# Maxima moved straight from the turned tile into the query rows, and 24 chunks ahead of a group's scores in place of 26

## The reference, cut to what matters

```python
x = x + attn_a(layernorm(x), Wq, bq, Wk, bk, Wv, bv, Wo, bo)
x = x + ffn(layernorm(x), w_gate, w_up, w_down)
x = x + attn_b(layernorm(x), wq, wk, wv, wo)
x = x + ffn(layernorm(x), w_gate, w_up, w_down)

# attn_a: 32 heads of 8 columns, no mask
scores = einsum('bhqd,bhkd->bhqk', q, k) * scale        # scale = 1/sqrt(8)
ctx    = einsum('bhqk,bhkd->bhqd', softmax(scores), v)  # then ctx @ Wo + bo
# attn_b: 32 query heads, 8 heads of keys and values (4 query heads share one)
amask  = where((j >= i - 128) & (j < i), -1e10, 0)      # a masked band
# ffn: silu(x @ w_gate) * (x @ w_up); of each 4 neighbours the 2 largest by size stay; @ w_down
```

## Time and profile before

| | us |
|---|---|
| median of 3 runs | 1660.44 |
| lowest, highest | 1656.22, 1662.11 |
| the profiled execution | 1661.54 |
| its span | 1659.6 |
| PE busy | 1611.3 (97%) |
| VectorE busy | 1490.8 (90%) |
| ScalarE busy | 1282.2 (77%) |
| POOL busy | 267.5 (16%) |
| mean busy share of the DMA queue's 16 engines | 29.2% |

### The profile page before, as it was taken

The page is one execution under the profiler, slowest core; times in us unless marked ns, Lnnn a source line. Parts: engine busy times, 40 slices in busy tenths (PEclk is TensorE's granted clock), DMA queues, the critical chain, the costliest instruction groups (busy, mean ns, idle before and its releaser), DMA issues.

```text
span 1659.6 us, 39596 instructions
## 1 busy us (share of the span) xinstructions
PE 1611.3 (97%) x14128; PEld 638.9 (38%) x14128; DVE 1490.8 (90%) x2168; ACT 1282.2 (77%) x2424; POOL 267.5 (16%) x623
## 2 busy tenths in 40 slices
PE   6899999999999999999988999999999999999999
PEld 3322222222222223777753222222222222247777
DVE  6999999999999997787777999999999999938765
ACT  3399999999999998433224999999999999983321
POOL 1410000000000000000012223333322233320000
PEclk9999999999999999999997999999999999999999
DMA  6943344334354321200404322222223222111000
GB/s 161 295 99 70 63 77 83 63 65 84 68 141 87 71 60 44 64 1 1 117 15 132 64 60 57 51 58 60 55 55 67 63 51 52 55 53 55 14 13 26
DMA packets 72126, 114.70 MB, mean 69 GB/s; under 512 B 12464, under 2 KB 27824, under 8 KB 71984
## 3 DMA queue, kind: packets, MB, share of 16 engines
q1 hardware_dynamic: 71984, 112.63, 29.2%
HBM read 71.96 MB, written 40.63 MB: 68 GB/s over the span
## 4 chain that ended last, share of the span: by engine, by line
PE 56%; DVE 32%; issue 7%; DMA 2%; ACT 1%; SPq 1%; DVEq 0%; POOLq 0%; ACTq 0%
DVE mneg L1305 28%; PE psum L785 18%; PE psum L767 11%; PE psum L737 7%; PE psum L887 6%; PE psum L843 6%; PE psum L848 3%; PE psum L700 2%; PE psum L823 2%; DVE area L1355 1%; PE psum L682 1%; PE psum L720 1%; DMA area<-k_stacks 0%; DVE stats L1198 0%; SPq L461 0%
## 5 line engine op out<-in xcount | busy, mean ns | idle before, releaser
L1055 ACT ACTIVATE area<-psum 128x512 f32<-128x512 f32 x2048 | 1097.2, 600 | 42.1 <-PE psum L767 14.6
L785 PE MATMUL psum<-area 128*32 128x256 f32 x8192 | 655.4, 392 | 0.4 <-POOL area L1567 0.4
L767 PE MATMUL psum<-area 51*128 51x512 bf16 x2048 | 638.9, 385 | 2.4 <-DVE vsb_b L1255 1.4
L1311 DVE CUSTOM_DVE_ANT_0 xn<-psum,band 128x1024 f32<-128x1024 f32 x512 | 588.4, 1235 | 12.6 <-PE psum L737 11.3
L1305 DVE TENSOR_REDUCE mneg<-psum 128x1 f32<-128x1024 f32 x512 | 581.0, 1209 | 7.1 <-PE psum L737 7.1
L785 PEld LDWEIGHTS psum<-area 128*32 128x32 f32 x8192 | 162.0, 108 | 400.9 <-issue 259.2
L737 PE MATMUL psum<-area 48*128 48x512 bf16 x1024 | 301.2, 386 | 8.0 <-DVE mneg L1305 4.6
L767 PEld LDWEIGHTS psum<-area 51*128 51x128 bf16 x2048 | 141.1, 94 | 426.5 <-ACT area L1055 353.6
L737 PE MATMUL psum<-k_max_b,area 48*128 48x512 bf16 x1024 | 292.5, 385 | 6.1 <-DVE mneg L1311 5.0
L1548 POOL TENSOR_TENSOR mparts<-mneg,nought 128x16 bf16<-128x16 f32 x64 | 14.2, 222 | 741.6 <-DVE mneg L1305 500.5
L1100 ACT ACTIVATE area<-psum 128x512 f32<-128x512 f32 x64 | 38.2, 600 | 120.0 <-PE psum L848 119.9
(11 more groups left out here) (89 smaller groups left out, 1096.8 us busy)
## 6 DMA issues: line engine op xcount, KB each, us to landing
ctx_rows<-area SPq DMA_DIRECT2D x64, 256.0 KB, 2.1
area<-q_stacks SPq DMA_DIRECT2D x32, 384.0 KB, 6.8
area<-k_stacks SPq DMA_DIRECT2D x64, 192.0 KB, 5.5
area<-q_stacks_b SPq DMA_DIRECT2D x32, 384.0 KB, 5.2
area<-q_stacks SPq DMA_DIRECT2D x32, 192.0 KB, 4.5
area<-q_stacks_b SPq DMA_DIRECT2D x32, 192.0 KB, 3.5
area<-ctx_rows SPq DMA_DIRECT2D x16, 256.0 KB, 3.9
area<-inv_rows SPq DMA_DIRECT2D x16, 256.0 KB, 4.6
```

Of the source, the lines that this page charges most:

```text
L767: pe.matmul(psum[:, BANK_OF["exp", g, u, head], :], k_st[lo:lo + ROWS + PARTS, buf, 0 if a else head // 2, kt * P:(kt + 1) * P], q_st[lo:l ...
L785: mm = pe.matmul(psum[head * VW:(head + 1) * VW, BANK_OF["ctx", g, qh], cols], vaug[:, buf, kt, head, :], probs[:, u % PRING, head, cols], ...
L1055: act.activation(probs[:, u % PRING, head, :], psum[:, BANK_OF["exp", like, u, head], :], ACT.Exp, scale=SCALE).then_inc(bank_freed, 1)
L1311: dve.tensor_tensor_reduce(band_out[:, c % 2, :], slot, band[:, at:at + SEQ], 1.0, -3.0e38, ALU.add, ALU.max, mneg[:, qh, col:col + 1]).th ...
```

## The change

SHIFT is 4 and TURN 6, so LEAD is 24: 24 chunks ahead of the first score, splits with units 4 and 12, turns with units 6 and 14, chunks in the last group's first four units. The last one or two V projections stand one chunk earlier. `mT` goes into the query rows without DRAM: for each parity one transfer of 24 rows of 128 into three rows of `q_st`. For that, `q_st` is laid out by query half, and the queries' rows are loaded by half, in twice as many transfers (96 increments of `st_loaded` for a group and buffer in place of 64, counted by the same rule). `mrow_stored` and `max_rows` are gone; ScalarE's copy into `mT` waits for `mrow_loaded` of two moves before. `ctx_stored` becomes one semaphore for each half.

```diff
-SHIFT = 3
-TURN = 5
+SHIFT = 4
+TURN = 6
 LEAD = CHUNKS - 2 * SHIFT
...
-        max_rows = dram("max_rows", (2, HALF, 2, PARTS, GH // 2 * BANK), BF16)
...
-        q_st, at = carve(at, [2, GH // 2, SEQ], BF16)
+        q_st, at = carve(at, [2, HALF, GH // 2, BANK], BF16)
...
-        V_CHUNKS = [(1, 5, CPH + 1, CPH + 3, CPH + 5, CPH + 7), (CPH + 3, CPH + 5, CPH + 7, CPH + 8)]
+        V_CHUNKS = [(1, 5, CPH + 1, CPH + 3, CPH + 5, CPH + 6), (CPH + 2, CPH + 4, CPH + 6, CPH + 7)]
...
-                    sp.dma_start(q_st[lo:lo + ROWS, buf, :, :],
-                                 qs[g, par::2].rearrange("a d k t -> (d k) a t")).then_inc(st_loaded[buf], 16)
+                    for qh in range(HALF):
+                        tokens = slice(qh * BANK, (qh + 1) * BANK)
+                        sp.dma_start(q_st[lo:lo + ROWS, buf, qh, :, :],
+                                     qs[g, par::2, :, :, tokens].rearrange("a d k t -> (d k) a t")
+                                     ).then_inc(st_loaded[buf], 16)
...
             def move_max(a, g, buf, qh):
                 n = HALF * (GROUPS * a + g) + qh
                 sp.wait_ge(bank_freed, turn_event(a, g, qh) + 1)
-                if not isinstance(g, int) or n >= 4:
-                    sp.wait_ge(mrow_loaded, 32 * (n - 3))
-                sp.dma_start(max_rows[buf, qh].rearrange("a c (i t) -> (a c i) t", t=P),
-                             mT[:, qh, :]).then_inc(mrow_stored, 16)
-                sp.wait_ge(mrow_stored, 16 * (n + 1))
+                if not isinstance(g, int) or n:
+                    sp.wait_ge(mrow_loaded, 32 * n)
                 for par in range(2):
-                    lo = PAR * par + ROWS
-                    sp.dma_start(q_st[lo:lo + PARTS, buf, :, qh * BANK:(qh + 1) * BANK],
-                                 max_rows[buf, qh, par].rearrange("c (i t) -> c i t", i=GH // 2)
-                                 ).then_inc(mrow_loaded, 16)
+                    lo, rows = PAR * par + ROWS, PARTS * CPH // 2
+                    sp.dma_start(q_st[lo:lo + PARTS, buf, qh, :, :],
+                                 mT[rows * par:rows * (par + 1), qh, :]).then_inc(mrow_loaded, 16)
...
-                          q_st[lo:lo + ROWS + PARTS, buf, head // 2, qh * BANK:(qh + 1) * BANK],
+                          q_st[lo:lo + ROWS + PARTS, buf, qh, head // 2, :],
...
-                    act.wait_ge(mrow_stored, 16 * (n - 1))
+                    act.wait_ge(mrow_loaded, 32 * (n - 1))
...
-                if not isinstance(g, int) or n >= 2:
-                    act.wait_ge(ctx_stored, 16 * (n - 1))
+                if not isinstance(g, int) or G:
+                    act.wait_ge(ctx_stored[qh], 16 * G)
```

More of the change, by code:

```diff
@@ L309, in hybrid_kernel @@
         st_loaded = [sem(f"stack_loaded{i}") for i in range(2)]
-        mrow_stored = sem("mrow_stored")
         mrow_loaded = sem("mrow_loaded")
-        ctx_stored = sem("ctx_stored")
+        ctx_stored = [sem(f"ctx_stored{i}") for i in range(HALF)]
         sums_loaded = sem("sums_loaded")
@@ L377, in hybrid_kernel @@
         w_a = [[wqkvo[0], wqkvo[1], wqkvo[2], wqkvo[3]], [wqo_b[0], wkv_b[0], wkv_b[1], wqo_b[1]]]
-        STACK_DMAS = 64
+        MAX_DMAS, ST_DMAS = 64, 96
         V_EARLY = 2
-        V_CHUNKS = [(1, 5, CPH + 1, CPH + 3, CPH + 5, CPH + 7), (CPH + 3, CPH + 5, CPH + 7, CPH + 8)]
+        V_CHUNKS = [(1, 5, CPH + 1, CPH + 3, CPH + 5, CPH + 6), (CPH + 2, CPH + 4, CPH + 6, CPH + 7)]
         V_TILES = BT // len(V_CHUNKS[1])
@@ L402, in stored, with loads @@
             return SD * SLOT[:pairs].count(slot)
-        def loads(G, buf):
-            return STACK_DMAS // 2 * (G - buf) + STACK_DMAS
+        def loads(G, buf, each):
+            return each // 2 * (G - buf) + each
         block = ctx.enter_context(nc.Block())
@@ L536, in move_max @@
                 sp.wait_ge(bank_freed, turn_event(a, g, qh) + 1)
-                if not isinstance(g, int) or n >= 4:
-                    sp.wait_ge(mrow_loaded, 32 * (n - 3))
-                sp.dma_start(max_rows[buf, qh].rearrange("a c (i t) -> (a c i) t", t=P),
-                             mT[:, qh, :]).then_inc(mrow_stored, 16)
-                sp.wait_ge(mrow_stored, 16 * (n + 1))
+                if not isinstance(g, int) or n:
+                    sp.wait_ge(mrow_loaded, 32 * n)
                 for par in range(2):
-                    lo = PAR * par + ROWS
-                    sp.dma_start(q_st[lo:lo + PARTS, buf, :, qh * BANK:(qh + 1) * BANK],
-                                 max_rows[buf, qh, par].rearrange("c (i t) -> c i t", i=GH // 2)
-                                 ).then_inc(mrow_loaded, 16)
+                    lo, rows = PAR * par + ROWS, PARTS * CPH // 2
+                    sp.dma_start(q_st[lo:lo + PARTS, buf, qh, :, :],
+                                 mT[rows * par:rows * (par + 1), qh, :]).then_inc(mrow_loaded, 16)
             def store_ctx(a, g, qh):
                 sp.wait_ge(bank_freed, ctx_event(a, g, qh) + 1)
-                sp.dma_start(ctx_rows[a][g, :, :, qh * BANK:(qh + 1) * BANK], ctx_sb[:, qh, :]).then_inc(ctx_stored, 16)
+                sp.dma_start(ctx_rows[a][g, :, :, qh * BANK:(qh + 1) * BANK], ctx_sb[:, qh, :]).then_inc(ctx_stored[qh], 16)
             def group(a, g, buf, first=False, ahead=2):
@@ L633, in _ @@
                     group(a, 2 * i + 2, 0)
-                sp.wait_ge(ctx_stored, 16 * (HALF * (GROUPS * a + GPB) + 1))
+                sp.wait_ge(ctx_stored[0], 16 * (GROUPS * a + GPB + 1))
+                sp.wait_ge(ctx_stored[1], 16 * (GROUPS * a + GPB))
                 load_sums(a, 0)
@@ L647, in _ @@
                 store_ctx(a, GROUPS - 1, 1)
-                sp.wait_ge(ctx_stored, 16 * HALF * GROUPS * (a + 1))
+                for qh in range(HALF):
+                    sp.wait_ge(ctx_stored[qh], 16 * GROUPS * (a + 1))
                 load_sums(a, 1)
@@ L729, in max_scores @@
                 if c == 0:
-                    pe.wait_ge(max_loaded[buf], loads(GROUPS * a + g, buf))
+                    pe.wait_ge(max_loaded[buf], loads(GROUPS * a + g, buf, MAX_DMAS))
                     if in_feed(a, g, c):
@@ L761, in scores @@
                 if head == 0 and u == 0:
-                    pe.wait_ge(st_loaded[buf], loads(GROUPS * a + g, buf))
+                    pe.wait_ge(st_loaded[buf], loads(GROUPS * a + g, buf, ST_DMAS))
                 if head == 0 and kt == 0:
@@ L1067, in copy_ctx @@
             def copy_ctx(a, g, qh, like):
-                n = HALF * (GROUPS * a + g) + qh
-                act.wait_ge(pv_done, UNITS * (GROUPS * a + g) + (qh + 1) * BT)
-                if not isinstance(g, int) or n >= 2:
-                    act.wait_ge(ctx_stored, 16 * (n - 1))
+                G = GROUPS * a + g
+                act.wait_ge(pv_done, UNITS * G + (qh + 1) * BT)
+                if not isinstance(g, int) or G:
+                    act.wait_ge(ctx_stored[qh], 16 * G)
                 act.copy(ctx_sb[:, qh, :], psum[:, BANK_OF["ctx", like, qh], :]).then_inc(bank_freed, 1)
@@ L1092, in silu_and_size @@
                 if c == 0 and h == 0:
-                    act.wait_ge(ctx_stored, 16 * HALF * GROUPS * (f + 1))
+                    for qh in range(HALF):
+                        act.wait_ge(ctx_stored[qh], 16 * GROUPS * (f + 1))
                 for r in range(5):
```

## The result

The changed kernel takes 1663.79 us (median of 22 runs, 1661.08 to 1665.81), the kernel before 1661.01 us beside it (22 runs, 1656.22 to 1662.57). The ratio is 1.0020, 95% interval 1.0014 to 1.0026: 2.8 us slower. The interval leaves 1 out, so the kernel is slower, by less than the 0.3% from which the prediction would have called it a difference. Forecast were 1660.9 us and a range of 1655.5 to 1666.5. The profiled execution has a span of 1663.1 us and a mean granted clock of 0.986 (before: 1659.6 and 0.989).

The account below looks back on a forecast made before the run. VectorE's unbroken stream of maxima was taken to bound the first attention, with its end behind VectorE's division. First attention +1.25 and second -0.75 made +0.5 us: 1660.9 us against the median, range 1655.5 to 1666.5.

Parts of the forecast that it names:

- The bounding engine: Middle of the first attention: VectorE's 479 maxima run without a hole, 542.04 of 542.05 us; their start sets the end.
- Start of the first attention: First score 0.87 us earlier, but chunk 33 at 92.7, so the stream of maxima is 1.25 us late.
- until the clock returns at 90.7: First attention's start: TensorE runs at 1.96 us a step at the lower clock until 90.7.
- End of the first attention: Stream, inverse, split and division move by +1.25 us; TensorE waits longer at unit 10, nothing is gained: +1.25 us.
- Second attention: Earlier first score and inverse's load, one unit less at the end: -0.75 us, bounds -3.5 and +1.5.
- My account of the inverse's load: Second attention's end: load issued at 1462.5 behind one transfer in place of two, allowing the tile at 1468.45.
- The move: Maxima into the query rows: 3.62 us from turn to landing, 4.6 us of room, 1.0 left; costs nothing.
- The query rows by half: Loads in each group: up to 7 us more of transfer, hidden at both bounds; 0 taken.
- B: Attention starts: the clock returns earlier or does not fall; -1.75 us in the first, total 1657.9 or 1655.2; chance 0.20.
- C: Steady groups: the move misses unit 8 or unit 0 and TensorE stalls; likely +7 us, 1668; chance 0.14.
- D: Both attentions' ends: the unit's gain reaches both, first not held by the division; -0.95 and -0.75, 1658.7; chance 0.08.

Follow-up runs that it names:

- second pair: Kernels after and before, each executed once more unchanged for a second trace: 1662.48 and 1660.45 us.
- after's second trace: The changed kernel executed once more, unchanged: 1662.48 us.
- after with the earlier division: The changed kernel with the first division of the context ahead of the last two of eight weight-splitting operations: 1658.48 us, ratio 0.9993.
- first pair: First traces of the unchanged kernels after and before, with spans of 1663.1 and 1659.6 us.
- before with the earlier division: The kernel before with the first division of the context ahead of the last two of eight weight-splitting operations: 1658.24 us, ratio 0.9981.
- the move alone: The changed kernel with 26 chunks ahead again, keeping the direct move and loads by half: 1660.47 us, ratio 1.0002.
- the two hops: The kernel before with 24 chunks ahead, the maxima still moved through DRAM: 1697.41 us, ratio 1.0219.

## Why the prediction was right in its range, and where its sum was not

The measured 1663.79 us lies in the range of 1655.5 to 1666.5, which the rivals had made wide, and inside the forecast's own 1658 to 1664. The loss of 2.8 us was forecast as 0.5, and the sum held less well than the range.

**The bounding engine** was read rightly: the stream of 479 maxima stands unchanged, moved as a whole.

**Start of the first attention.** First score 78.45 forecast, 78.47 measured; first exponential 80.2 and 80.24; unit 2 at 83.5 and 83.73; steps of 1.96 and 1.98 us. Chunk 33 was forecast for 92.7; it came at 94.50 in one execution and 92.18 in the other. The step "until the clock returns at 90.7" was a fixed number for something that isn't fixed. The size of 1.25 us seems to hold in the second pair (1.44), but that is luck: 0.89 us of it stood between the two executions beforehand. Measured from the copy of V behind chunk 21 the stream is late by 3.13 us where the stretch is 13.7 us long and by 0.44 and 0.22 where it is 6.8 (after's second trace, after with the earlier division); no trace of after has the 10.2 us that the forecast assumed.

**End of the first attention.** This is the step that failed: a term put at nothing. I wrote that TensorE waits for the division at unit 10 "only longer (1.31 + 2.26 us)" and that nothing more follows. The wait was right, 3.57 forecast and 3.22 and 3.20 measured. But I gave it no price beyond itself, and it has one: the granted clock falls to the lower level in the last microsecond of the wait and stays there for 6.8 us, which puts the end of the attention 2.45 us later than the tile in the first pair (5.39 - 2.94) and 2.48 in the second (3.74 - 1.26). Without this term the two pairs, measured from the copy of V, are +1.0 and -1.2 us, around my +0.5, but that is partly luck: the start gave +3.13 and +0.44 in place of +1.25, and the second attention -2.01 and -1.60 in place of -0.75. The earlier division, which takes the wait away, takes the stretch away too. The Trainium skill, "TensorE: Matmul & The Clock Gate", section What's actually happening, has the rule that I had cited for one direction alone: the low clock is the default and activity releases it. By it a longer wait is a risk in itself, and these traces agree: at this place 1.2 to 1.3 us of waiting left the clock alone, 2.50 and 3.2 us did not.

**Second attention.** -0.75 forecast, -2.01 and -1.60 measured. The unit less at the end was worth 2.36 us in the first pair (2.10 forecast): from the end of the stream to the last product with V it is 30.22 us (1461.93 to 1492.15) where it was 32.58. The stream was late by 0.35 us in place of 1.35, since the first score came 1.68 us sooner after the first attention's end (227.15 us against 228.83) and not 0.6; the second pair has the same 227.15 against 228.86. Before shows 6.8 us of low clock at 875.7 just ahead of it, after 3.4 at 882.6, in both pairs. Two other traces have it the other way round: before with the earlier division has 3.4 us of it and 227.89 us to the first score, after with the earlier division has 6.8 us and 228.21. So the lead is worth 0.6 to 0.7 us here (228.83 to 228.21, 227.89 to 227.15), as forecast, and the other 0.9 to 1.1 us go with the stretch and aren't the change's. Where the stretches are alike, all from the first attention's end on gives 0.1 to 0.5 us (821.70 against 822.18 and 821.82) and 0.3 (820.17 against 820.47), less than my 0.75. My account of the inverse's load was wrong: I had it issued at 1462.5, behind one transfer in place of two, and it is issued behind the move of the maxima, as before, at 1467.12. The division ended at 1472.78 and TensorE was there only at 1473.32, so that the error cost nothing.

**The move.** 3.62 us forecast from the turn to the last landing, 3.3 to 3.5 measured; room 4.6 and 4.64; nobody waits. The Trainium skill's 512 bytes ("DMA: Bandwidth & Descriptors", section Specifications) spoke against rows of 256 bytes ending in SBUF. No price of it can be seen: the move alone has the time of before, 1.0002 (0.9993 to 1.0012).

**The query rows by half.** 0 forecast, 0 by the same run. My upper bound was taken from the wrong row: the 384 KB of the earlier trace rows are the loads for the maxima, which the change leaves as they are (6.8 us before, 7.0 after). The loads that were halved had 192 KB and landed after 4.5 us; now they have 96 KB and land after 3.3. The pages of before and after, issues (KB each, median us to landing):

```profile
area<-q_stacks SPq DMA_DIRECT2D x32, 192.0 KB, 4.5
...
area<-q_stacks SPq DMA_DIRECT2D x64, 96.0 KB, 3.3
```

**The rivals.** B (the clock comes back sooner) is what the first start looks like in after's second trace, 6.8 us in place of 10.2, and not in its first, 13.7. The stream gained nothing by it (0.44 us late), so B's price of -1.75 us did not come even there. C (the move misses its unit) did not happen, but does with the two hops, at 36 us and not 7. D (the gain of a unit reaches the first end) was barred by the division, as forecast; the kernel after with the earlier division is D's condition made true, and behind the stream it gains what D has it gain, a unit of 2.0 us. That its time of 1658.48 us is also D's price of 1658.7 is luck: it was measured on another chip, and its terms against before are others (2.4 and 1.7 us at the first attention's end in place of 0.95, 0.1 to 0.5 in the second in place of 0.75).

## What to carry to other kernels

A wait that only grows is not free on TensorE: look at the granted clock behind it, and price both (here 3.2 us of waiting and 2.5 us of slower work). Where two engines meet at an end, first take the waited-for work out from behind work that nobody needs yet (here two splitting operations behind a division: 2.8 us in the kernel before, 5.3 in the one after), and only then shorten the other side. At the start of a stage fill TensorE's idle time with matmuls for nobody, but no more than fit into it: seven took 3.29 us and brought the first start no gain in the kernel before, and four and three in place of seven and five were worth 2.4 us by the traces. Before two traces are compared, look at a row ahead of the change: 0.9 us stood between two of them there.

## What the runs showed of the hardware that I had not expected

The length of a low stretch at the same place of the same kernel is not the same in each execution (13.7 and 6.8 us), and times go with it. Mean time of the runs by their mean granted clock:

| clock | 0.984 | 0.985 | 0.986 | 0.987 | 0.988 | 0.989 | 0.990 |
|---|---|---|---|---|---|---|---|
| after (22 runs) | 1665.8 | 1664.9 | 1664.3 | 1663.6 | 1662.1 | - | - |
| before (29 runs) | - | - | - | - | 1662.4 | 1661.2 | 1658.2 |

The 29 runs of before are those beside the experiments in the kernel before, on chip 9; the record has no clocks for the 22 beside after. At the one clock that both have, 0.988, they take the same time (5 and 3 runs). That fits a loss made of low clock, and doesn't prove it. One trace of each kernel can show more or less than the 2.8 us between the medians: the first pair shows 3.5 in the span, the second 2.1.

The Trainium skill, in the same section on the clock, has it that the number of matmuls at the lower level at a kernel's start varies from run to run; the two traces show the same of a start in the middle of a kernel.
